# A fused attention, state-space and expert kernel: values and keys projected in four column blocks, with edits in the opening, the state-space stage and the experts

## The chip, the cores and the metric

The kernel is one program on one core of a Trainium2 chip. Its time is the device time of one launch in microseconds, beginning to end. The engines are PE (TensorE, matrix products; its weight loads are listed as PEld), DVE (VectorE), ACT (ScalarE), POOL (GpSimd) and SP (SyncE, which here only issues DMAs).

## The reference, cut to what matters

```python
# x: (16, 64, 128), ctx: (16, 1601, 128), all float32
q = layernorm(x) @ Wq.T + bq                   # 16 heads of 8
k, v = ctx @ Wk.T + bk, ctx @ Wv.T + bv
x = x + (softmax(q @ k.T / sqrt(8)) @ v) @ Wo.T + bo       # head by head
u = layernorm(layernorm(x)) * ln1_w + ln1_b
z, xBC, dt = in_proj(u); xs, Bm, Cm = silu(causal_conv4(xBC))
h = exp(dt * A) * h + dt * xs (x) Bm;  y = h . Cm + D * xs   # a scan over 64 tokens, 4 heads of 64
x1 = layernorm(x) + rmsnorm(y * silu(z)) @ out_proj
x = x + x1 + mlp(layernorm(x1))                # 512 wide, gelu
w = softmax(top2(dist(x, centroid)))           # 8 experts, each 342 wide
x = x + sum_e w_e * ((silu(x @ Wg + bg) * (x @ W1 + b1)) @ W2 + b2)
```

## The kernel before, in words

**Precision.** Products that must be exact to about float32 are made of three bf16 products (`product3`: high by high, high by low, low by high), the high and low halves made by ACT or POOL.

**Tiling.** The context of one batch lies as 128 features by 1601 tokens. Attention runs in 16 rounds, one a batch, of 13 steps, one for each 128 tokens of the context. In step k of round i, PE computes the scores of the 128 tokens (`scores`, eight matmuls, four groups of heads by two halves), ACT takes their exponentials into `probs`, and two steps later PE multiplies `probs` with the values and adds up in `sums` (`sum_values`): 16 float32 matmuls, four groups of four that write four different blocks of 32 columns of the array. The softmax needs each query's maximum before its scores, so a further pair of matmuls, a unit of `maxima`, makes 802 of the scores of batch i + 1 or i + 2 in a PSUM buffer and DVE reduces it (line 880); there are 16 units a batch. `turn_max` turns the maxima, DVE makes shifts of them, and these go into the rows of `q_cur` by DMA.

**The buffers handed to and fro.** `wide` is one PSUM tensor with two slots of 1024 columns. Everything that PE makes for another engine beside scores takes the two slots in turn; `RING` (from `ring_order`) numbers the uses, and `half_free` makes PE wait until the use before last was emptied. A slot is filled with a unit of maxima (emptied by DVE, about 1 us), half of the values of batch i + 2 (`vals`, 7 or 6 blocks of 128 tokens, 21 or 18 matmuls; copied by DVE), half of the keys of batch i + 3 (`keys`, two blocks of 401 tokens, six matmuls; copied by ACT), or a turn. `V_STEPS = (2, 5)`, `K_STEPS = (6, 8)` (9 and 11 in round 0) say in which steps they come: in the order of a step, scores, the first unit, the sum, further units, values, turn, keys.

**The opening.** Before round 0 the keys and values of batches 0 and 1, the keys of batch 2 and all queries are made. `score` and `sums` are not yet in use and serve as four spare PSUM banks: `make_spare` fills them in the order `SPARE_FIRST`, then `SPARE_LATER`, whose first 12 entries stand one behind each unit of maxima of batch 0 and whose last four (the keys of batch 2, emptied by ACT) stand behind the turn. The DMA that brings the shift of batch 0 into `q_cur` is issued by ACT's queue.

**Other queues.** POOL splits each context (2.9 and 3.2 us) and each batch's keys into high and low halves, in program order. SP issues in fixed steps the next context's load (`C_STEP`), and the copies of the split keys into `k_stack` (`H_STEP`, `L_STEP`), 1.6 MB and more a round. The program itself also comes over DMA: the page's queues q8 and q14 have the kind "instruction".

**State-space and MLP stage.** `mamba_mlp` works on tiles of two batches (128 tokens). DVE scans gains of 1024 elements four times (`gain`, line 1516), multiplies them with the product of Cm and Bm into `mix` (line 1525), PE sums `dtx` by `mix` (line 1224), DVE adds D * xs (line 1538) and multiplies with the gate.

**Experts.** A half of an expert is 512 tokens. For each of three blocks of 114 hidden units PE makes gate and up (`up`, six bf16 matmuls of 512 columns), ACT takes silu, DVE the product `hid_e`; and 12 float32 matmuls of 128 columns (24 records in the trace, since each passes twice) bring the half before down (`finish`, in two parts, line 1698), which DVE weighs and adds. Experts 1 to 6 run in a loop of two.

## Time and profile before

| | us |
|---|---|
| median of 3 runs (608.32 to 609.47) | 608.58 |
| the profiled execution, and its span | 609.61, 607.8 |
| opening, to the first scores | 55.8 |
| 16 attention rounds | 346.8 |
| state-space and MLP, with the routing | 87.2 |
| experts | 118.0 |
| busy: PE, PEld | 533.9, 353.5 |
| busy: DVE, ACT, POOL | 424.9, 358.3, 257.7 |

The mean granted clock of PE is 0.94 of 2.4 GHz. How the rows below are read. A window has its start and end, its length, the busy time and number of instructions of PE, PEld, DVE, ACT and POOL, PE's granted clock as a share, the busy share of the DMA engines (summed from modelled times, so it can pass 1), and GB/s. A row of the timeline has start, length, engine, line, operation, what is written and read, the shape, how many instructions were put together, and in brackets the idle time before it with what ended it; "issue" is idle time in which the engine waited for nothing that the profile shows. A row of the page's part 5 has a group's busy time, the mean of one in ns, the idle time before its instructions and what ended most of it. A DMA queue's row has packets, megabytes, and time as a share of 16 engines' span. Matmuls overlap: in a row of several the starts and not the lengths say how fast they pass.

### The profile page before, as it was taken

To read this page: it belongs to the slowest core of one execution; us is meant where nothing else is said; L and a number is where in the kernel's file an instruction comes from. 1 tells how busy PE (TensorE), PEld (TensorE's weight loads), DVE (VectorE), ACT (ScalarE), POOL (GpSimd) and SP (SyncE) were. 2 spreads that over 40 slices of the span, in tenths; PEclk is the share of its full clock that TensorE was granted. 3 is DMA by queue.
4 is the path that set the end of the run, shared out by engine and by line. 5 is a ranking of instruction groups with operands and counts; after the bars stand their busy time and mean duration, and the time that the engine had idled before them with its cause. 6 is when DMAs were issued, how large, how long until landed. Compare 5 with 4: busy or idle time off the path is not lost. (4 is left out here: it accounts for less than half of the span.)

```text
span 607.8 us, 17717 instructions
## 1 busy us (share of the span) xinstructions
PE 533.9 (88%) x7478; PEld 353.5 (58%) x7478; DVE 424.9 (70%) x754; ACT 358.3 (59%) x655; POOL 257.7 (42%) x137
## 2 busy tenths in 40 slices
PE   2795899999998899999999889977676979999997
PEld 1532655665565565566556556644465647777786
DVE  5174877888787788888878778347898565455454
ACT  4773476777677678777767759854813533233231
POOL 2694966658567467655854497022002000000000
PEclk9785899999999999999999889988758979999999
DMA  7794936965784684595557381011000000000001
GB/s 212 114 153 73 187 46 96 141 81 92 108 109 76 96 116 78 88 139 76 92 60 108 82 133 39 2 44 53 1 1 0 1 1 1 1 1 0 0 0 35
DMA packets 16405, 41.57 MB, mean 68 GB/s; under 512 B 3990, under 2 KB 6814, under 8 KB 16218
## 3 DMA queue, kind: packets, MB, share of 16 engines
q1 hardware_dynamic: 15592, 40.09, 40.2%
q8 instruction: 56, 0.92, 0.8%
q10 hardware_dynamic: 740, 0.42, 0.2%
q14 instruction: 17, 0.14, 0.1%
HBM read 19.70 MB, written 0.52 MB: 33 GB/s over the span
## 5 line engine op out<-in xcount | busy, mean ns | idle before, releaser
L880 DVE TENSOR_REDUCE half_max<-wide 128x2 f32<-128x802 f32 x256 | 241.7, 989 | 60.1 <-PE wide L570 56.4
L806 ACT ACTIVATE probs<-score 128x512 f32<-128x512 f32 (+1 forms) x416 | 225.8, 596 | 67.0 <-PE score L621 66.6
L641 PE MATMUL sums<-probs,values 128*32 128x192 f32 (+3 forms) x3328 | 133.4, 279 | 3.9 <-issue 3.9
L641 PEld LDWEIGHTS sums<-probs,values 128*32 128x32 f32 (+1 forms) x3328 | 87.2, 109 | 57.8 <-issue 27.3
L570 PE MATMUL wide<-k_stack,q_cur 48*128 48x401 bf16 x512 | 89.0, 346 | 8.8 <-issue 4.2
L621 PE MATMUL score<-q_cur,k_stack 50*128 50x128 bf16 (+1 forms) x1664 | 84.3, 221 | 12.0 <-ACT probs L806 5.0
L621 PEld LDWEIGHTS score<-q_cur,k_stack 50*128 50x128 bf16 (+1 forms) x1664 | 51.5, 96 | 43.5 <-issue 14.5
L1753 ACT ACTIVATE gate<-gu,gate_bias 114x512 f32<-114x512 f32 x48 | 32.9, 687 | 68.3 <-PE gu L1719 65.1
L405 POOL TENSOR_TENSOR ctx_hi<-ctx_in,one 128x1601 bf16<-128x1601 f32 x15 | 42.9, 2859 | 70.5 <-PE wide L492 61.7
L1838 DVE SCALAR_TENSOR_TENSOR hid_e<-gu,keep_bgu,gate 114x512 f32<-114x512 f32 x48 | 36.0, 751 | 51.9 <-ACT gate L1753 51.9
L417 POOL TENSOR_TENSOR k_hi<-k_full,one 128x1601 bf16<-128x1601 f32 x15 | 42.9, 2857 | 52.9 <-ACT k_full L788 38.6
L1698 PEld LDWEIGHTS down<-keep_w,hid_e 114*128 114x128 f32 x384 | 47.6, 192 | 3.6 <-DVE hid_e L1838 0.4
L408 POOL TENSOR_TENSOR ctx_lo<-ctx_in,ctx_hi 128x1601 bf16<-128x1601 f32 x15 | 48.6, 3243 | 1.2
L420 POOL TENSOR_TENSOR k_lo<-k_full,k_hi 128x1601 bf16<-128x1601 f32 x15 | 48.5, 3236 | 1.2
L1698 PE MATMUL down<-keep_w,hid_e 114*128 (+1 forms) x384 | 47.9, 275 | 0.2 <-DVE hid_e L1838 0.2
L788 ACT ACTIVATE k_full<-wide,keep_vecs 128x802 f32<-128x802 f32 x26 | 24.2, 930 | 31.6 <-PE wide L492 31.6
L570 PEld LDWEIGHTS wide<-k_stack,q_cur 48*128 48x128 bf16 x512 | 25.2, 95 | 28.4 <-DVE half_max L880 15.7
L876 DVE COPY values<-wide 128x896 f32<-128x896 f32 (+1 forms) x28 | 28.7, 1025 | 15.8 <-PE wide L492 15.8
L1717 PE MATMUL gu<-keep_t_hi,keep_w_hi 128*114 128x512 bf16 x96 | 37.2, 388 | 1.8 <-DVE hid_e L1838 1.8
L490 PE MATMUL wide<-wkv_hi,ctx_hi 128*128 128x128 bf16 x182 | 33.2, 224 | 4.3 <-DVE half_max L880 4.3
L1719 PE MATMUL gu<-keep_t_hi,keep_w_lo 128*114 128x512 bf16 x96 | 36.8, 384 | 0.0
L1718 PE MATMUL gu<-keep_t_lo,keep_w_hi 128*114 128x512 bf16 x96 | 36.8, 384 | 0.0
(290 smaller groups left out, 725.4 us busy)
## 6 DMA issues: line engine op xcount, KB each, us to landing
k_stack<-k_hi SPq DMA_DIRECT2D x64, 204.0 KB, 6.4
ctx_in<-in_ctx SPq DMA_DIRECT2D x56, 200.1 KB, 6.2
k_stack<-k_lo SPq DMA_DIRECT2D x32, 204.0 KB, 8.6
ctx_in<-in_wgu SPq DMA_DIRECT2D x16, 171.0 KB, 4.4
keep_w<-in_w SPq DMA_DIRECT2D x1, 1368.0 KB
ctx_in<-in_ctx SPq DMA_DIRECT2D x1, 800.5 KB, 8.4
keep_x<-in_x SPq DMA_DIRECT2D x1, 512.0 KB, 6.8
out<-keep_x SPq DMA_DIRECT2D x2, 256.0 KB, 2.3
```

Of the source, the lines that this page charges most:

```text
L405: pool.tensor_tensor(ctx_hi[:, n, 0:LK], ctx_in[:, n, :], one[:].to_broadcast([P, LK]), ALU.mult).then_inc(s_splithi, 1)
L408: pool.tensor_tensor(ctx_lo[:, n, 0:LK], ctx_in[:, n, :], ctx_hi[:, n, 0:LK], ALU.subtract).then_inc(s_split, 1)
L417: pool.tensor_tensor(k_hi[:, 0:LK], k_full[:, 0:LK], one[:].to_broadcast([P, LK]), ALU.mult).then_inc(s_khi, 1)
L420: pool.tensor_tensor(k_lo[:, 0:LK], k_full[:, 0:LK], k_hi[:, 0:LK], ALU.subtract).then_inc(s_klo, 1)
L570: last = pe.matmul(wide[:, w, 512 * p:512 * p + CH], q_cur[half:half + TERM, b % NQ, g].rearrange("p h q -> p (h q)"), k_stack[half:half + ...
L621: last = pe.matmul(score[0:m, (2 * step + p) % NSCORE, P * g:P * g + P], k_stack[half:half + TERM + 2, n, g, k * P:k * P + m], q_cur[half: ...
L641: last = pe.matmul(sums[32 * g:32 * g + 32, first * LQ:(first + heads) * LQ], values[0:m, n, k, VW * g + 2 * c:VW * g + 2 * c + 32], probs ...
L806: nc.scalar.activation(probs[0:m, step % NPROB, :].rearrange("r (g p c) -> r p g c", g=G, p=2)[:, p], score[0:m, (2 * step + p) % NSCORE, ...
L880: dve.tensor_reduce(half_max[:, b % 2, :, u // 4, u % 4], wide[:, w, :].rearrange("p (c k) -> p c k", c=2)[:, :, 0:CH], AX.X, ALU.max).the ...
L1698: last = pe.matmul(down[:, h, P * t:P * t + P], hid[:, h, n, P * t:P * t + P], keep.w2[:, bass.ds(e, 1), n, :].rearrange("p e c -> p (e c) ...
L1717: pe.matmul(o, hi, t_hi[:, half], start=True, stop=False)
L1718: pe.matmul(o, hi, t_lo[:, half], start=False, stop=False)
```

## The change

- **Values and keys in the rounds.** `keys` and `vals` call `columns3` instead of `product3`: each matmul of 128 output columns of the array becomes four of 32, that write four blocks of 32 partitions. Each output is made of the same three products in the same order. `make_spare` in the opening keeps `product3`.
- **Order in a step.** Values and keys stand after the sum and ahead of a step's further units of maxima. Values of batch 2 move from round 0 to the time between the turn of batch 0 and the first scores.
- **Opening.** The queries' first two groups come ahead of the maxima, and the last four spare jobs, the keys of batch 2, stand behind units 12 to 15 of the maxima and no longer behind the turn.
- **State-space stage.** Tokens of one batch only see each other, so the two batches of a tile are laid one under the other: gains, scan and mix have 64 columns where they had 128. The term D * xs becomes matmuls with a diagonal matrix ahead of the sums (`skipped`), the sum of the squares on POOL becomes two matmuls, and a scan's start is set by a bias on ACT and no longer by memsets on POOL.
- **Experts.** ACT makes the high half of `hid_e` (`high`), POOL the low half (`low`) and the halves of w2 (`split`), and the down product becomes 36 bf16 matmuls for a half of an expert in place of 12 float32 ones; its two parts stand at other places in the stream.

The core of the diff:

```diff
-    order += [("m", 0, u) for u in range(16)] + [("t", 0, 0)]
+    order += [("m", 0, u) for u in range(16)] + [("t", 0, 0), ("v", 2, 0), ("v", 2, 1)]
     for i in range(B):
         for k in range(NK):
-            order += [("m",) + unit for unit in units_at(i, k)]
-            if k in V_STEPS and i + 2 < B:
+            order += [("m",) + unit for unit in units_at(i, k)[:1]]
+            if k in V_STEPS and 0 < i < B - 2:
                 order += [("v", i + 2, V_STEPS.index(k))]
+            order += [("k",) + half for half in keys_at(i, k)]
+            order += [("m",) + unit for unit in units_at(i, k)[1:]]
             if k == turn_step(i) and i + 1 < B:
                 order += [("t", i + 1, 0)]
-            order += [("k",) + half for half in keys_at(i, k)]
...
+            def columns3(out, lhs_hi, lhs_lo, rhs_hi, rhs_lo):
+                for n, (lhs, rhs) in enumerate(((lhs_hi, rhs_hi), (lhs_hi, rhs_lo), (lhs_lo, rhs_hi))):
+                    for c in range(4):
+                        at = slice(32 * c, 32 * c + 32)
+                        last = pe.matmul(out[at], lhs[:, at], rhs, start=(n == 0), stop=(n == 2))
+                return last
...
-                    last = product3(wide[:, w, 512 * c:512 * c + CH], wkv_hi[:, 0, :], wkv_lo[:, 0, :],
+                    last = columns3(wide[:, w, 512 * c:512 * c + CH], wkv_hi[:, 0, :], wkv_lo[:, 0, :],
...
-                    last = product3(wide[:, w, at:at + P], ctx_hi[:, n, ks], ctx_lo[:, n, ks],
+                    last = columns3(wide[:, w, at:at + P], ctx_hi[:, n, ks], ctx_lo[:, n, ks],
...
                 maxima(0, u)
-                if u < 12:
+                if u < 10:
                     make_spare(SPARE_LATER[u])
+                elif u >= 12:
+                    make_spare(SPARE_LATER[u - 2])
             pe.wait_ge(s_nident, 16)
             turn_max(0)
-            for what in SPARE_LATER[12:]:
-                make_spare(what)
+            for half in range(2):
+                vals(2, half)
...
+                    if k in V_STEPS and 0 < i < B - 2:
+                        vals(i + 2, V_STEPS.index(k))
+                    for half in keys_at(i, k):
+                        keys(*half)
                     for unit in units[1:]:
                         maxima(*unit)
-                    if k in V_STEPS and i + 2 < B:
-                        vals(i + 2, V_STEPS.index(k))
                     if k == turn_step(i) and i + 1 < B:
                         turn_max(i + 1)
-                    for half in keys_at(i, k):
-                        keys(*half)
...
+            for half in range(2):
+                vals_out(2, half)
...
-            for h in range(2):
-                pool.wait_ge(s["ysq"], 2 * h + 2)
-                pool.tensor_tensor(y_sq[:, 0, half(h)], y_sq[:, 0, half(h)], y_sq[:, 1, half(h)],
-                                   ALU.add).then_inc(s["yss"], 1)
...
+            def skipped(h2):
+                pe.wait_ge(s["bcc"], 4)
+                pe.wait_ge(s["silu"], 4 * h2 + 2)
+                for b in range(2):
+                    for c in range(2):
+                        pe.matmul(y_out(h2, b, c), keep.skip[:, c, :],
+                                  xbc[:, c, half(h2)].rearrange("p (t b q) -> p t b q", b=2, q=LQ)[:, :, b, :],
+                                  start=(c == 0), stop=False, skip_group_check=True)
+            skipped(0)
             for h2 in range(2):
-                pe.wait_ge(s["bcc"], 4)
-                pe.wait_ge(s["dtx"], 4 * h2 + 4)
                 for t in range(4):
                     pe.wait_ge(s["mix"], 4 * h2 + t + 1)
+                    pe.wait_ge(s["dtx"], 4 * h2 + t + 1)
                     for h in range(MH):
                         r = 64 * (h % 2)
-                        last = pe.matmul(ps[r:r + 64, YA_SLOT[h2], 512 * (h // 2) + P * t:512 * (h // 2) + P * t + P],
-                                         dtx[:, 4 * h2 + t, 64 * h:64 * h + 64], mix[:, 4 * h2 + t, h, :],
-                                         start=True, stop=True)
+                        for b in range(2):
+                            rows = slice(LQ * b, LQ * b + LQ)
+                            last = pe.matmul(y_out(h2, b, h // 2)[r:r + 64, t, :],
+                                             dtx[rows, 4 * h2 + t, 64 * h:64 * h + 64], mix[rows, 4 * h2 + t, h, :],
+                                             start=False, stop=True, skip_group_check=True)
                 last.then_inc(s["ya"], 1)
+                if h2 == 0:
+                    skipped(1)
...
+                if c == 1:
+                    nc.scalar.activation(root_of[:], ones[:], ACT.Sqrt)
...
-                    count(dve.scalar_tensor_tensor(out=y[:, c, half(h)], in0=xbc[:, c, half(h)],
-                                                   scalar=vecs[:, V_D + c:V_D + c + 1],
-                                                   in1=ps[:, YA_SLOT[h], half(c)], op0=ALU.mult, op1=ALU.add))
-                    settle()
-                    dve.tensor_tensor(y[:, c, half(h)], y[:, c, half(h)], zg[:, c, half(h)],
-                                      ALU.mult).then_inc(s["yc"], 1)
+                    def by_batch(buf):
+                        return buf[:, c, half(h)].rearrange("p (t b q) -> p b t q", b=2, q=LQ)
+                    got = ps[:, YA_SLOT[h], :].rearrange("p (b c t q) -> p c b t q", b=2, c=2, q=LQ)[:, c]
+                    dve.tensor_tensor(by_batch(y), got, by_batch(zg), ALU.mult).then_inc(s["yc"], 1)
...
+        hid_hi = sb("hid_hi", [HT, 2, 2, NH, 512], BF16)
+        hid_lo = sb("hid_lo", [HT, 2, 2, NH, 512], BF16)
+        w2_hi = sb("w2_hi", [HT, E, NH, P], BF16)
+        w2_lo = sb("w2_lo", [HT, E, NH, P], BF16)
...
+                        hi, lo = hid_hi[:, par, h, n, P * t:P * t + P], hid_lo[:, par, h, n, P * t:P * t + P]
+                        pe.matmul(o, hi, w_hi2[:, n, :], start=(n == 0), stop=False)
+                        pe.matmul(o, hi, w_lo2[:, n, :], start=False, stop=False)
+                        last = pe.matmul(o, lo, w_hi2[:, n, :], start=False, stop=(n == NH - 1))
...
+                    if n == 0 and before:
+                        finish(*before, 1)
+                    if n == NH - 1 and prev:
+                        finish(*prev, 0)
...
+            def split(e):
+                got = of_expert(keep.w2, e)
+                pool.tensor_tensor(of_expert(w2_hi, e), got, one[:].unsqueeze(2).to_broadcast([HT, NH, P]),
+                                   ALU.mult).then_inc(s["w2s"], 1)
+                pool.wait_ge(s["w2s"], e * 2 + 1)
+                pool.tensor_tensor(of_expert(w2_lo, e), got, of_expert(w2_hi, e), ALU.subtract).then_inc(s["w2s"], 1)
+            def low(e, h, par, prev, before):
+                for n in range(NH):
+                    pool.wait_ge(s["hi"], e * 6 + (3 * h + n + 1))
+                    if isinstance(e, int) and e == E - 1 and h == 1 and n == NH - 1:
+                        return
+                    pool.tensor_tensor(hid_lo[:, par, h, n, :], hid[:, n, :], hid_hi[:, par, h, n, :],
+                                       ALU.subtract).then_inc(s["lo"], 1)
+                if h == 1 and not isinstance(e, int):
+                    split(e + 1)
...
+            def high(e, h, par, n):
+                act.wait_ge(s["hid"], e * 6 + (3 * h + n + 3))
+                nc.scalar.copy(hid_hi[:, par, h, n, :], hid[:, n, :]).then_inc(s["hi"], 1)
...
+                    if n:
+                        high(e, h, par, n - 1)
+                    elif prev:
+                        high(*prev, NH - 1)
```

The order of PE in step 5 of round 1, from the scores of the step to the first product of the half of values (`wide<-wkv_hi,ctx_hi`; `sums` is the sum, `wide<-k_stack` a unit of maxima), before:

```order
L621 MATMUL score<-q_cur,k_stack 128x128 x8
L570 MATMUL wide<-k_stack,q_cur 128x401 x2
L641 MATMUL sums<-probs,values 32x192 x4
L641 MATMUL sums<-probs,values 32x64 x4
L570 MATMUL wide<-k_stack,q_cur 128x401 x2
L490 MATMUL wide<-wkv_hi,ctx_hi 128x128
L491 MATMUL wide<-wkv_lo,ctx_hi 128x128
L492 MATMUL wide<-wkv_hi,ctx_lo 128x128
```

and of the change:

```order
L635 MATMUL score<-q_cur,k_stack 128x128 x8
L584 MATMUL wide<-k_stack,q_cur 128x401 x2
L655 MATMUL sums<-probs,values 32x192 x4
L655 MATMUL sums<-probs,values 32x64 x4
L505 MATMUL wide<-wkv_hi,ctx_hi 32x128 x4
L505 MATMUL wide<-wkv_lo,ctx_hi 32x128 x4
L505 MATMUL wide<-wkv_hi,ctx_lo 32x128 x4
```

The second unit of maxima has gone behind the values, and each product is four matmuls of 32 columns.

PE at the end of the opening, from the twelfth unit of batch 0 on (`score` and `sums` are spare banks here: `xnT,wq` a group of queries, `ctx_hi,wkv_hi` one quarter of the keys of batch 2; `wide<-nident` is the turn), before:

```order
L570 MATMUL wide<-k_stack,q_cur 128x401 x2
L536 MATMUL score<-xnT,wq 128x512
L570 MATMUL wide<-k_stack,q_cur 128x401 x8
L578 MATMUL wide<-nident,row_max 16x128
L490 MATMUL score<-ctx_hi,wkv_hi 128x401
L491 MATMUL score<-ctx_lo,wkv_hi 128x401
L492 MATMUL score<-ctx_hi,wkv_lo 128x401
L490 MATMUL sums<-ctx_hi,wkv_hi 128x401
```

and of the change:

```order
L584 MATMUL wide<-k_stack,q_cur 128x401 x2
L550 MATMUL score<-xnT,wq 128x512
L584 MATMUL wide<-k_stack,q_cur 128x401 x6
L496 MATMUL score<-ctx_hi,wkv_hi 128x401
L497 MATMUL score<-ctx_lo,wkv_hi 128x401
L498 MATMUL score<-ctx_hi,wkv_lo 128x401
L584 MATMUL wide<-k_stack,q_cur 128x401 x2
L496 MATMUL sums<-ctx_hi,wkv_hi 128x401
L497 MATMUL sums<-ctx_lo,wkv_hi 128x401
L498 MATMUL sums<-ctx_hi,wkv_lo 128x401
L584 MATMUL wide<-k_stack,q_cur 128x401 x2
```

The four quarters of keys, behind the turn before, stand between the last units of maxima.

PE in the first expert's part ahead of the loop (`gu` gate or up, `down` the down product), before:

```order
L1718 MATMUL gu<-keep_t_lo,keep_w_hi 114x512
L1719 MATMUL gu<-keep_t_hi,keep_w_lo 114x512
L1717 MATMUL gu<-keep_t_hi,keep_w_hi 114x512
L1718 MATMUL gu<-keep_t_lo,keep_w_hi 114x512
L1719 MATMUL gu<-keep_t_hi,keep_w_lo 114x512
L1698 MATMUL down<-keep_w,hid_e 128x128 x6
L1717 MATMUL gu<-keep_t_hi,keep_w_hi 114x512
L1718 MATMUL gu<-keep_t_lo,keep_w_hi 114x512
```

and of the change:

```order
L1753 MATMUL down<-w_hi,hid_hi 128x128
L1754 MATMUL down<-w_lo,hid_hi 128x128
L1755 MATMUL down<-w_hi,hid_lo 128x128
L1772 MATMUL gu<-keep_t_hi,keep_w_hi 114x512
L1773 MATMUL gu<-keep_t_lo,keep_w_hi 114x512
L1774 MATMUL gu<-keep_t_hi,keep_w_lo 114x512
L1772 MATMUL gu<-keep_t_hi,keep_w_hi 114x512
L1773 MATMUL gu<-keep_t_lo,keep_w_hi 114x512
L1774 MATMUL gu<-keep_t_hi,keep_w_lo 114x512
L1753 MATMUL down<-w_hi,hid_hi 128x128
L1754 MATMUL down<-w_lo,hid_hi 128x128
```

Between the groups of six first products stood six float32 matmuls at a time; now the down products stand in groups of three bf16 ones for each block, and in other gaps.

## Rows read from the trace of the kernel before

**Rows 1.** Windows by stage: engines' busy time (count), granted clock, DMA share, GB/s

```profile
0.00:55.80 55.80, 35.42 (x180) 17.61 (x180) 26.36 (x53) 31.98 (x74) 29.32 (x22) 0.80 0.74 141
55.80:402.60 346.80, 322.47 (x6246) 204.95 (x6246) 272.89 (x361) 249.53 (x457) 217.97 (x100) 0.98 0.59 91
...
489.80:607.80 118.00, 112.04 (x704) 86.89 (x704) 59.46 (x153) 36.18 (x61) 0.00 (x0) 0.98 0.02 5
```

**Rows 2.** Part 5 of the page, costliest group of VectorE

```profile
L880 DVE TENSOR_REDUCE half_max<-wide 128x2 f32<-128x802 f32 x256 | 241.7, 989 | 60.1 <-PE wide L570 56.4
```

**Rows 3.** Timeline, PE, a step and the step after

```profile
222.80 0.40 PE L621 MATMUL score<-q_cur,k_stack 50*128 50x128 bf16 x8
223.03 0.34 PE L570 MATMUL wide<-k_stack,q_cur 48*128 48x401 bf16 x2
223.29 0.64 PE L641 MATMUL sums<-probs,values 128*32 128x192 f32 x16
223.87 0.23 PE L490 MATMUL wide<-wkv_hi,ctx_hi 128*128 128x128 bf16 x1
...
224.98 0.23 PE L621 MATMUL score<-q_cur,k_stack 50*128 50x128 bf16 x2
225.56 0.34 PE L621 MATMUL score<-q_cur,k_stack 50*128 50x128 bf16 x6 [0.35 <-issue]
```

**Rows 4.** Timeline, PE, at a stop

```profile
202.82 0.53 PE L641 MATMUL sums<-probs,values 128*32 128x192 f32 x7
204.52 0.43 PE L641 MATMUL sums<-probs,values 128*32 128x192 f32 x9 [1.17 <-issue]
```

**Rows 5.** Windows between stops, of a block, and of a quiet stretch

```profile
183.72:204.52 20.80, 18.86 (x382) 12.05 (x382) 17.70 (x22) 15.09 (x28) 12.36 (x6) 1.00 0.61 89
204.52:225.56 21.04, 19.63 (x383) 12.47 (x383) 16.40 (x21) 14.82 (x27) 12.37 (x7) 1.00 0.60 88
197.20:204.52 7.32, 6.08 (x131) 3.98 (x132) 6.55 (x7) 4.34 (x8) 1.97 (x1) 1.00 1.06 135
336.60:358.46 21.86, 20.44 (x382) 12.59 (x382) 17.58 (x21) 15.09 (x28) 16.20 (x8) 0.92 0.57 90
372.60:378.00 5.40, 5.40 (x138) 3.54 (x130) 5.07 (x7) 4.80 (x10) 3.78 (x2) 1.00 0.02 5
```

**Rows 6.** Part 3 of the page, and the DMA view of 200.80 to 202.70

```profile
q8 instruction: 56, 0.92, 0.8%
...
q8 instruction: 1, 0.02, 6.0%
```

**Rows 7.** Windows, one round in two parts

```profile
258.30:272.30 14.00, 13.28 (x265) 8.74 (x264) 11.67 (x15) 9.73 (x19) 7.84 (x5) 1.00 0.99 142
272.30:279.90 7.60, 7.26 (x143) 4.20 (x138) 6.14 (x10) 6.20 (x12) 6.19 (x3) 1.00 0.06 19
```

**Rows 8.** Timeline, PE in the experts; then part 5 of the page

```profile
528.83 1.50 PE L1698 MATMUL down<-keep_w,hid_e 114*128 x12
530.17 0.38 PE L1717 MATMUL gu<-keep_t_hi,keep_w_hi 128*114 128x512 bf16 x1
...
L1753 ACT ACTIVATE gate<-gu,gate_bias 114x512 f32<-114x512 f32 x48 | 32.9, 687 | 68.3 <-PE gu L1719 65.1
L408 POOL TENSOR_TENSOR ctx_lo<-ctx_in,ctx_hi 128x1601 bf16<-128x1601 f32 x15 | 48.6, 3243 | 1.2
```

**Rows 9.** Timeline, state-space stage: DVE, then PE

```profile
441.14 2.28 DVE L1516 TENSOR_TENSOR_SCAN gain<-decay_all,keep_delta 128x1024 f32<-128x1024 f32 x1
443.45 1.28 DVE L1525 TENSOR_TENSOR mix<-gain,ps 128x512 f32<-128x512 f32 x2
...
453.97 0.75 DVE L1538 SCALAR_TENSOR_TENSOR y<-xbc,keep_vecs,ps 128x512 f32<-128x512 f32 x1
...
450.42 5.48 PE L1224 MATMUL ps<-mix,keep_sums 128*64 128x128 f32 x64
```

**Rows 10.** Timeline, PE, the first scores

```profile
55.82 0.39 PE L621 MATMUL score<-q_cur,k_stack 50*128 50x128 bf16 x4 [3.12 <-DMA q_cur<-shift]
```

More of the change, by code:

```diff
@@ L985, in _ @@
                             row_maxima(b)
-                    if k in V_STEPS and i + 2 < B:
+                    if k in V_STEPS and 0 < i < B - 2:
                         vals_out(i + 2, V_STEPS.index(k))
+                    for b, u in units[1:]:
+                        maximum(b, u)
+                        if u == 15:
+                            row_maxima(b)
                     if k == turn_step(i) and i + 1 < B:
@@ L1056, in mamba_mlp @@
         names = ("w turn o ot otc att x1 st var sq u ln vt vtc dtp dts dte mm conv silu zin zsil "
-                 "ones dp dpt dpc tsp cen dots tap bc bcc bc0 scan cb mix xt dtx ya yc ysq yss out r rq y1 "
+                 "ones dp dpt dpc tsp cen dots tap bc bcc scan cb mix xt dtx ya yc ysq out r rq y1 "
                  "fc gelu pr")
@@ L1176, in spread @@
                     for h in range(MH):
-                        last = pe.matmul(ps[:, BC_SLOT[c], P * (MH * t + h):P * (MH * t + h) + P],
-                                         sel[:, h, :], decayT[:, tok(2 * c + t)], start=True, stop=True)
+                        at = LQ * (MH * t + h)
+                        for b in range(2):
+                            first = P * (2 * c + t) + LQ * b
+                            last = pe.matmul(ps[LQ * b:LQ * b + LQ, BC_SLOT[c], at:at + LQ],
+                                             sel[:, h, 0:LQ], decayT[:, first:first + LQ], start=True, stop=True)
                 last.then_inc(s["bc"], 1)
@@ L1200, in overlap @@
                 for t in range(4 * h, 4 * h + 4):
-                    last = pe.matmul(ps[:, CB_SLOT, tok(t)], xbc[0:64, 2, tok(t)], xbc[0:64, 3, tok(t)],
-                                     start=True, stop=True)
+                    for b in range(2):
+                        first = P * t + LQ * b
+                        last = pe.matmul(cb_out(t)[LQ * b:LQ * b + LQ, :],
+                                         xbc[0:64, 2, first:first + LQ], xbc[0:64, 3, first:first + LQ],
+                                         start=True, stop=True)
                 last.then_inc(s["cb"], 1)
@@ L1236, in _ @@
                                          start=(c == 0), stop=(c == 1))
-                pe.wait_ge(s["yss"], h + 1)
+                pe.wait_ge(s["ysq"], 2 * h + 2)
                 for t in range(4 * h, 4 * h + 4):
-                    last = pe.matmul(bank(6 + h)[:, t:t + 1], y_sq[:, 0, tok(t)], ones[:], start=True, stop=True)
+                    for c in range(2):
+                        last = pe.matmul(bank(6 + h)[:, t:t + 1], y_sq[:, c, tok(t)], ones[:],
+                                         start=(c == 0), stop=(c == 1))
                 last.then_inc(s["out"], 1)
@@ L1325, in _ @@
             gate_silu(0)
+            act.wait_ge(s["ones"], 1)
             for c in range(4):
@@ L1622, in experts @@
         small = pb("small", [P, 2, 512])
-        names = "w gb sp nrm rt top te sel weT wtc gu gate hid down acc b2"
+        names = "w one gb sp nrm rt top te sel weT wtc gu gate hid hi lo w2s down acc b2"
         s = {n: sem("e_" + n) for n in names.split()}
@@ L1657, in per_expert, with of_expert @@
             body(E - 1, 1, False)
+            last()
+        def of_expert(buf, e):
+            return buf[:, bass.ds(e, 1)].rearrange("p e n c -> p (e n) c")
         @block.sync
@@ L1720, in up, with last_ones, _ @@
                     last.then_inc(s["gu"], 1)
-                    if between and n:
-                        between(n - 1)
-            per_expert(pe, up, finish, route)
+                    if n == 0 and before:
+                        finish(*before, 1)
+                    if n == NH - 1 and prev:
+                        finish(*prev, 0)
+            def last_ones():
+                finish(E - 1, 0, 1, 1)
+                finish(E - 1, 1, 1, 0)
+                finish(E - 1, 1, 1, 1)
+            per_expert(pe, up, last_ones, route)
+        @block.gpsimd
+        def _(pool):
+            pool.memset(one[:], 1.0).then_inc(s["one"], 1)
+            pool.wait_ge(s["one"], 1)
+            def split(e):
[13 more added lines that the diff above has]
+                    split(e + 1)
+            pool.sem_inc(s["lo"], 3)
+            split(0)
+            split(1)
+            per_expert(pool, low, lambda: None, lambda step: None)
         @block.scalar
@@ L1740, in route, with gates @@
                                        small[0:E, h, :]).then_inc(s["wtc"], 1)
-            def gates(e, h, par, between):
+            def high(e, h, par, n):
+                act.wait_ge(s["hid"], e * 6 + (3 * h + n + 3))
+                nc.scalar.copy(hid_hi[:, par, h, n, :], hid[:, n, :]).then_inc(s["hi"], 1)
+            def gates(e, h, par, prev, before):
                 if h == 0:
@@ L1831, in weigh, with hidden @@
                 last.then_inc(s["acc"], 1)
-            def hidden(e, h, par, between):
+            def hidden(e, h, par, prev, before):
                 for n in range(NH):
```

116 lines of the change are left out of this document (65 added, 51 removed).

## The prediction

> **What bounds the kernel now.** I read first the stages by windows. The opening ends at 55.8, the attention rounds take the 346.8 us to 402.6 (57% of the span), the experts the last 118, and the state-space and MLP stage stands between them [rows 1]. The profiled execution took 609.61 us around a span of 607.8; the median of the runs shown is 608.58, so terms measured in the profile are taken off the median.
>
> In the rounds PE and DVE are both near full: 322.5 and 272.9 us of 346.8. The costliest group is DVE's row maxima, 989 ns each [rows 2], 16 a round: 15.8 us. With two copies of values of about 1 us each and the small work of a shift I estimate 18.9 us in a round; a round lasts 346.8 over 16, 21.7, the undisturbed ones 21.3. The order of time shows what PE does in a step: a score group, a pair of maxima and a sum of values take 1.08 us together (222.80 to 223.87) [rows 3]. Thirteen of these are 14.0 us; two halves of values (1.1 and 1.0), two of keys (six matmuls of 401 columns at 2.4 GHz, 1.03 each), three more maxima (0.26 each), and a turn with the changes of the array's shape (some 1.0) give about 19.9. So PE has some 1.6 us of room in a round and DVE some 2.5; neither alone is the bound, for they hand two buffers to and fro.
>
> The reader is then to see a wait of another kind. At 203 us PE stops inside a sum of values, in the middle of one group that waits for no semaphore, and goes on at 204.52; "issue" stands beside it [rows 4]. The same stands at 225.56 [rows 3]. Between those two ends PE ran 383 matmuls and 383 weight loads, 766 instructions; between the end at 183.72 and that at 204.52, 382 and 382 [rows 5]. The page has 56 packets of kind "instruction" with 0.92 MB, 16.4 KB each [rows 6]; 14,956 PE instructions over 56 is 267 to a packet. So PE's program comes in blocks of some 256 instructions, three to a stretch between stalls (768 against 764 and 766, the rest being branch and semaphore instructions), and a stall falls at a block's edge. The block of 197.20 to 204.52 took 7.32 us; its packet is on the queue only in the stretch from 200.80 to 202.70, 3.6 us after the edge at which it could first be wanted [rows 5, 6]. Data traffic explains the lateness: in the first 14 us of a round the DMA engines are 99% busy, in the rest 6% [rows 7]. With no traffic (372.60 to 378.00) 268 instructions pass in 5.4 us and nothing stalls [rows 5].
>
> **The change, part by part.**
>
> *Values and keys in four blocks of columns.* Each matmul of 128 columns becomes four of 32. In streaming nothing is lost: the sums of values are such groups of four already, and 16 of their matmuls pass in 0.58 us (223.29 to 223.87), where eight of 192 columns in two passes and eight of 64 would need 1.7 us one after another, so they do run beside each other [rows 3]. Half a step of values, 21 matmuls in 1.11 us, should become 84 in 1.1 to 1.2. The switches of shape beside a sum of values go away, about 0.09 us each (a pair of maxima streams 0.17 us and the sum starts 0.26 after it, 223.03 to 223.29), perhaps three a round, 0.3 us; since DVE and not PE closes the round, I count this as nothing.
>
> What grows is the program. A round has 39 matmuls of values and 12 of keys; they become 156 and 48, 153 more, and with their weight loads 306 more instructions on some 780 (764 and 766 in 20.80 and 21.04 us, scaled to 21.3). That is 4.3 blocks a round where 3.1 were. All of it falls in the first nine steps, just where DMA is busy: nine steps of 52 instructions (26 matmuls and their loads), 312 for the values and 96 for the keys are 876 in 13.9 us of PE work, so a block is used up in 4.1 us there, and one that is fetched in traffic needed 7.3 [rows 5, 7]. Each such block makes PE wait 3.2 us. Two such blocks fit into 14 us of traffic: 6.4 us a round, less the 1.6 of room, 4.8. If only one of them is that late, 1.6 remain. Twelve full rounds (the last ones load no values) give 19 to 58 us; I take the middle, 38. At the lower end outside this, the fetch stays hidden and the term is nothing.
>
> *Values of batch 2 ahead of the rounds, keys of batch 2 within the maxima, two query groups earlier.* PE waits at 55.82 for the shift's DMA for 3.12 us [rows 10], and that DMA was issued on ACT's queue behind the last four copies of keys. Now these copies come before the turn, and the values fill the wait. I take 4 us off the opening and 3 off round 0, which loses two halves of values at half clock: minus 7, between minus 10 and minus 3. Queued behind the moved keys is the rest of the maxima: were context 2 not split by then, DVE would stand idle with them.
>
> *State-space stage.* The scan goes from 1024 to 512 elements: 2.28 us each becomes 1.14; the mix pair 1.28 becomes about 0.8 [rows 9]. Four times 1.6 is 6.5 us of DVE. But PE's order of turns and overlaps stays and holds DVE up (each pair of turned tiles comes after its spread), so I count 3.5. The skip term leaves DVE (four of 0.75) [rows 9] and becomes eight float32 matmuls of 256 columns and four passes, 0.43 us each at 2.4 GHz and 0.85 at 1.2, on PE in line ahead of the sums, where the clock stood at half until about 453; the second half of the skip now also stands ahead of the first output projection. The 64 records of the old sum took 5.48 us [rows 9]; in quarters of the array they stream half as long. The sum on POOL goes, eight more one-column matmuls come, and a table load moves off the path. I count minus 2.5 in all, between minus 7 and plus 4.
>
> *Experts.* 12 down records take 1.34 us (528.83 to 530.17), and nothing on PE waits [rows 8]. A half of an expert costs 18 first products of 512 columns at 2.4 GHz, 0.216 each, 3.89, and 24 down records, 2.68: 6.57. Down becomes 36 bf16 matmuls of 128 columns at the 0.056 us at which the values' matmuls follow each other (21 from 223.87 to 224.98, less the switch) [rows 3], 2.0. ACT gains three copies, estimated at 0.6 each, beside three gates of 0.69: 3.9 of 5.9. DVE keeps what it has. POOL's three low parts and its share of the weights' split come to about 4.3, by its 3.24 us for 1601 elements [rows 8]. All stay under PE's 5.9. Sixteen halves give 0.67 each, 10.7, and a tail longer by the copy and the low part, about 0.5: minus 10, between minus 12 and minus 6.
>
> **The sum.** 608.6 - 7 - 2.5 - 10 + 38 = 627.
>
> **Rivals.**
> A. The blocks arrive in time. For it: only one block in three is late today, and a stall costs 1.5 us at most. Then the rounds stay at DVE's pace and the time is 608.6 - 19.5 = 589. The Trainium skill's page "Runtime: NRT & Kernel Launch", section "Instruction fetch mechanics", has this rule: the next block of 256 instructions is fetched while one is executed, and the cost of an edge is mostly hidden. By that rule alone the time would be this 589; rows 4 and 5 show edges that cost over a microsecond.
> B. No late blocks, but small matmuls have a floor from start to start. A score group's eight take 0.23 us (222.80 to 223.03), 29 ns each; a sum's 16 take 36 ns each [rows 3]. At 29 ns for every start the halves of values take 2.4 and 2.1 us, 2.4 us more a round, or 0.8 to 2.4 after the room: 10 to 31 us, 600 to 620, say 610. Against it: in groups of narrow blocks four starts seem to share one slot. The skill's page "TensorE: Matmul & The Clock Gate", section "Wait — 56ns, not 53.3ns?", gives about 25 ns as the least distance of two starts; by it 84 would take 2.1 us, and no row here shows a long run of narrow ones.
> C. Late blocks and, after them, half the clock. The stretch after the stall that ended at 336.60 ran at 0.92 of the clock [rows 5]. A dozen falls of about 1 us on top of the upper half of the term: 640 to 655.
> D. The opening's moved keys wait for the split of context 2 and the early gain is lost, with the rest as forecast: 634.
>
> **How the numbers follow.** My forecast 0.50, C 0.12, D 0.05, B 0.15, A 0.18. What a measurement of this kernel can tell from no change is 0.2%, 1.2 us. Faster is A and the low part of B: 0.20. Same: 0.03. Slower: 0.77. The range runs from 597, which leaves out A, to 648, which takes in most of the term's upper end. The forecast's own range is 610 to 646.
>
> **What would show it.** The rounds' stage should take some 380 us instead of 346.8, with over 20 waits of PE marked "issue" of 1 to 3 us, nearly all in the first two thirds of a round, and 71 to 75 instruction packets instead of 56. Windows between these waits should hold multiples of 256 instructions. DVE's idle time before its maxima should grow by the same 35 us. An experts' half should take 5.9 us; the first score should come near 52. The forecast is wrong if the rounds last under 350 us with 70 and more packets (A), or if the value halves themselves stretch evenly to 2 us (B).

## The result, and the profile after

The changed kernel takes 658.94 us, median of 4 runs (655.08 to 660.43), against 609.03 for the kernel before on the same chip: 1.080 times as long, 95% interval 1.074 to 1.086. The forecast was 627, its range 597 to 648.

The stages by windows in the changed kernel (columns as in [rows 1]); the last two windows are a half of an expert in the loop, and the experts' first 15.4 us from the first product on:

```profile
0.00:52.12 52.12, 33.80 (x372) 18.26 (x372) 27.56 (x54) 31.37 (x74) 32.28 (x23) 0.93 0.82 157
52.12:462.20 410.08, 336.77 (x8197) 215.91 (x8196) 273.24 (x362) 249.69 (x458) 216.49 (x101) 0.92 0.48 77
462.20:544.90 82.70, 66.01 (x492) 45.54 (x493) 56.51 (x183) 39.13 (x64) 6.87 (x11) 0.78 0.05 18
544.90:657.20 112.30, 103.35 (x896) 74.26 (x896) 64.00 (x154) 60.88 (x109) 68.13 (x64) 0.96 0.02 6
...
581.88:587.78 5.90, 5.90 (x57) 4.30 (x55) 3.36 (x8) 3.58 (x7) 4.10 (x4) 1.00 0.00 0
546.60:562.00 15.40, 12.80 (x57) 7.01 (x58) 8.66 (x37) 8.26 (x16) 7.25 (x7) 0.79 0.01 2
```

Against [rows 1] the opening is 3.7 us shorter, the rounds are 63.3 us longer, the state-space and MLP stage 4.5 us and the experts 5.7 us shorter: 49.4 us longer in all, as the spans have it (657.2 and 607.8). So the rounds alone make the loss. In them DVE is busy for 273.24 us as before (272.89), its maxima take as long as before, and PE has 14 us more of busy time; most of what grew is time in which PE and DVE stand still, and the granted clock fell from 0.98 to 0.92.

The waits of PE in the changed kernel, largest first (us in total, times, longest), then rows of the page: DVE's maxima, its copies of values (L876 before, L892 after), and three of the DMA queues:

```profile
PE wide L505 <- issue: 24.1, 11, 4.3
PE sums L655 <- issue: 19.9, 6, 4.6
PE score L635 <- issue: 9.7, 3, 3.9
```

```profile
L896 DVE TENSOR_REDUCE half_max<-wide 128x2 f32<-128x802 f32 x256 | 243.0, 989 | 85.0 <-PE wide L584 81.0
...
L876 DVE COPY values<-wide 128x896 f32<-128x896 f32 (+1 forms) x28 | 28.7, 1025 | 15.8 <-PE wide L492 15.8
L892 DVE COPY values<-wide 128x896 f32<-128x896 f32 (+1 forms) x28 | 28.7, 1024 | 49.7 <-PE wide L505 49.7
...
q8 instruction: 75, 1.23, 0.9%
q10 hardware_dynamic: 740, 0.42, 0.2%
q14 instruction: 19, 0.15, 0.1%
```

Twenty waits for nothing that the profile shows, 53.7 us; nineteen of them, 51.5 us, lie in the rounds, and one of 2.25 at the end of the opening. The kernel before had seven in its rounds, 6.9 us, the longest 1.6. There are 75 packets of q8 where [rows 6] has 56. DVE's wait before the maxima grew by 24.9 us (85.0 for the 60.1 of [rows 2]) and that before its copies of values by 33.9 (49.7 for 15.8): it waits for what the stopped PE has not made (35 before the maxima alone had been forecast). That PE's stops stand at the edges of blocks of 256 instructions is to be read from two stops that follow one another and from the window between their ends:

```profile
251.89 0.23 PE L505 MATMUL wide<-wkv_hi,ctx_hi 128*32 128x128 bf16 x2 [3.62 <-issue]
...
272.92 0.51 PE L655 MATMUL sums<-probs,values 128*32 128x192 f32 x3
278.00 1.07 PE L655 MATMUL sums<-probs,values 128*32 128x192 f32 x13 [4.57 <-issue]
279.01 0.61 PE L635 MATMUL score<-q_cur,k_stack 50*128 50x128 bf16 x8
279.41 0.54 PE L584 MATMUL wide<-k_stack,q_cur 48*128 48x401 bf16 x2
```

```profile
251.89:278.00 26.11, 20.28 (x509) 12.66 (x510) 16.93 (x21) 14.82 (x27) 14.02 (x6) 0.91 0.50 74
```

It holds 509 matmuls and 510 loads, 1019 of the 1024 of four blocks (the rest are branch and semaphore instructions or missing records). The lateness of the packet shows in the DMA view. From 269.40, the edge before, to 274.60 there is only data on the queues, 103.4% of the engines' time; the packet comes in the stretch from 274.60 to 276.50:

```profile
q1 hardware_dynamic: 231, 0.61, 103.4%
```

```profile
q1 hardware_dynamic: 82, 0.24, 108.5%
q8 instruction: 1, 0.02, 5.8%
```

PE had used up its block at 273.4, in 4.0 us (the forecast's 4.1), stopped inside a sum of values, and went on at 278.00. Behind the stop the same instructions take longer: a score group passes in 0.40 us (279.01 to 279.41) and not in the 0.23 of [rows 3]. The clock was at its lower level, 1.2 GHz, in the whole of the first window below, and the second shows it back at 2.4:

```profile
276.70:283.50 6.80, 5.50 (x121) 4.00 (x120) 1.57 (x2) 1.13 (x3) 0.47 (x1) 0.50 0.23 54
...
283.50:290.30 6.80, 5.84 (x134) 3.39 (x132) 4.55 (x7) 5.31 (x9) 5.92 (x3) 1.00 0.22 60
```

And the narrow matmuls themselves, in a half of values at the full clock: four of them start in every 0.055 us, the pace at which the prediction has one of 128 columns pass (0.056). A half of values still takes some 1.2 us.

```profile
216.94 0.23 PE L505 MATMUL wide<-wkv_hi,ctx_lo 128*32 128x128 bf16 x4
217.00 0.23 PE L505 MATMUL wide<-wkv_hi,ctx_hi 128*32 128x128 bf16 x4
217.06 0.23 PE L505 MATMUL wide<-wkv_lo,ctx_hi 128*32 128x128 bf16 x4
217.11 0.23 PE L505 MATMUL wide<-wkv_hi,ctx_lo 128*32 128x128 bf16 x4
```

### The profile page after: what moved, and what is told of

It is laid out like the page before. It is cut to its first block and busy times, and to the rows that moved or that the text cites. A ratio compares the mean times of both kernels' runs of the same rounds, so it can differ in the third digit from the quotient of the medians.

```text
span 657.2 us, 22953 instructions
## 1 busy us (share of the span) xinstructions
PE 539.9 (82%) x9956; PEld 354.0 (54%) x9956; DVE 421.3 (64%) x751; ACT 381.1 (58%) x704; POOL 323.8 (49%) x197
## 5 line engine op out<-in xcount | busy, mean ns | idle before, releaser
L655 PE MATMUL sums<-probs,values 128*32 128x192 f32 (+3 forms) x3328 | 141.5, 292 | 21.7 <-issue 19.9
L655 PEld LDWEIGHTS sums<-probs,values 128*32 128x32 f32 (+1 forms) x3328 | 90.9, 114 | 81.5 <-issue 49.9
L584 PE MATMUL wide<-k_stack,q_cur 48*128 48x401 bf16 x512 | 92.9, 360 | 11.7 <-ACT k_full L804 6.3
L635 PE MATMUL score<-q_cur,k_stack 50*128 50x128 bf16 (+1 forms) x1664 | 88.0, 228 | 16.4 <-issue 9.7
L635 PEld LDWEIGHTS score<-q_cur,k_stack 50*128 50x128 bf16 (+1 forms) x1664 | 55.1, 99 | 44.1 <-issue 19.8
L1805 POOL TENSOR_TENSOR hid_lo<-hid_e,hid_hi 114x512 bf16<-114x512 f32 x47 | 54.1, 1157 | 36.2 <-ACT hid_hi L1833 35.2
L892 DVE COPY values<-wide 128x896 f32<-128x896 f32 (+1 forms) x28 | 28.7, 1024 | 49.7 <-PE wide L505 49.7
L505 PE MATMUL wide<-wkv_hi,ctx_hi 128*32 128x128 bf16 x728 | 39.3, 238 | 12.7 <-issue 9.8
L505 PE MATMUL wide<-wkv_lo,ctx_hi 128*32 128x128 bf16 x728 | 39.3, 238 | 6.3 <-issue 6.3
L505 PE MATMUL wide<-wkv_hi,ctx_lo 128*32 128x128 bf16 x728 | 38.9, 238 | 3.8 <-issue 3.8
L804 ACT ACTIVATE k_full<-wide,keep_vecs 128x802 f32<-128x802 f32 x26 | 24.1, 929 | 28.2 <-PE wide L505 28.2
```

Source lines behind the costliest of these rows:

```text
L505: last = pe.matmul(out[at], lhs[:, at], rhs, start=(n == 0), stop=(n == 2))
L584: last = pe.matmul(wide[:, w, 512 * p:512 * p + CH], q_cur[half:half + TERM, b % NQ, g].rearrange("p h q -> p (h q)"), k_stack[half:half + ...
L635: last = pe.matmul(score[0:m, (2 * step + p) % NSCORE, P * g:P * g + P], k_stack[half:half + TERM + 2, n, g, k * P:k * P + m], q_cur[half: ...
L655: last = pe.matmul(sums[32 * g:32 * g + 32, first * LQ:(first + heads) * LQ], values[0:m, n, k, VW * g + 2 * c:VW * g + 2 * c + 32], probs ...
L1805: pool.tensor_tensor(hid_lo[:, par, h, n, :], hid[:, n, :], hid_hi[:, par, h, n, :], ALU.subtract).then_inc(s["lo"], 1)
```

## The experiments

Theory F: the program's blocks come late behind the data of a round, and there are more of them. Rivals: the new order in a step (O), and the small matmuls by themselves, by their starts or by the clock (S). A second question came from the first runs: what a stop costs beyond its own length (theory H: the clock is at half for a while after it).

**e1_plain.** Plain products in keys and vals, the rest of the change kept.

```diff
-                    last = columns3(wide[:, w, 512 * c:512 * c + CH], ...
+                    last = product3(wide[:, w, 512 * c:512 * c + CH], ...
-                    last = columns3(wide[:, w, at:at + P], ctx_hi[:, n, ks], ...
+                    last = product3(wide[:, w, at:at + P], ctx_hi[:, n, ks], ...
```

> The changed kernel with product3 in keys and vals: no narrow blocks in the rounds, the rest of the change stays. Theory F (the program's blocks come late in the DMA traffic of a round, and there are more blocks): the stops go back to those of the kernel before, the rounds to 340 to 347 us, and with the opening, the state-space stage and the experts as in the profile after (3.7, 4.5 and 5.7 us shorter) the time is 589 to 596. Rival O (the new place of values and keys ahead of the second unit of maxima makes DVE and PE wait for each other): the rounds stay above 390 us, time 640 or more.

Measured 593.95 (592.99 to 595.24), ratio to before 0.973, 0.969 to 0.978. The rounds take 347.58 us with a clock of 0.98, and PE waits for "issue" 8.3 us:

```profile
PE sums L655 <- issue: 4.3, 4, 2.3
PE score L635 <- issue: 4.0, 2, 2.1
```

O falls as the cause of the loss. The rounds of the changed kernel are 62.5 us longer than these (410.08 less 347.58), 43.2 of them in stops (51.5 in its rounds, less 8.3).

**e2_before_columns.** The kernel before with `columns3` in the two calls, nothing else.

```diff
-                    last = product3(wide[:, w, ...
+                    last = columns3(wide[:, w, ...
```

> The kernel before with columns3 in keys and vals of the rounds and nothing else. Theory F: rounds of 400 to 415 us, some 20 stops marked issue of 1 to 5 us, 75 instruction packets less those of the other stages (about 72), time 660 to 672. Rival O: no more than 615, since the order is that of before.

Measured 676.48 (673.77 to 678.81), 1.110, 1.105 to 1.116: a little over the top of the expectation. The rounds take 408.6 us, with 48.8 us of "issue" in 18 waits at the three places shown. This one edit makes the whole loss; the rest of the change gains 14 to 18 us with it or without it (608.31 less 593.95, 676.48 less 658.94).

```profile
PE wide L499 <- issue: 20.5, 9, 4.7
PE sums L649 <- issue: 18.6, 6, 4.5
PE score L629 <- issue: 9.7, 3, 4.1
```

**e4_filler.** Plain products, and tiny matmuls that nobody reads make the program as long as the changed one.

```diff
+            def filler(w, blocks):
...
+                for n in range(9 * blocks):
+                    c = n % 4
+                    at = slice(32 * c, 32 * c + 32)
+                    last = pe.matmul(wide[at, w, 1016 + n // 4 % 4:1017 + n // 4 % 4], wkv_hi[:, 0, at],
+                                     wkv_hi[:, 1, 0:1], start=True, stop=True)
+                return last
```

> The changed kernel with product3 in keys and vals, and behind each half as many more tiny matmuls as columns3 would add (32 columns of the array, one column moving, into PSUM columns that nobody reads; 153 a round with their loads): the program has the length of the changed one, the streaming that of the plain one. Theory F: the stops come back, time 645 to 662. Rival S: within 10 us of the kernel with plain products, under 606.

Measured 675.59 (671.13 to 676.91), 1.108, 1.103 to 1.114. The stops come back, 41.3 us of them in rounds of 424.2, with work that streams almost nothing. That it is 17 us slower than the changed kernel had not been expected. An estimate from the trace: 63 fillers take 0.56 us (308.14 to 308.70, shape switch included), so 153 some 1.4 us a round and 18 us in all, where narrow blocks take no time more than wide ones. Its stops are 10 us less than the changed kernel's and its rounds 14 us longer, so the fillers explain most of the 24 us between and not all.

```profile
308.14 0.63 PE L513 MATMUL wide<-wkv_hi 128*32 128x1 bf16 x63
308.70 0.40 PE L647 MATMUL score<-q_cur,k_stack 50*128 50x128 bf16 x8
```

**e3_spread.** The changed kernel; SP issues a round's ten DMAs of 0.2 MB one a step.

```diff
-H_STEP, L_STEP, C_STEP = 1, 3, 5
+H_STEPS, L_STEPS, C_STEPS = (0, 1, 2, 3), (4, 5), (6, 7, 8, 9)
```

> The changed kernel with the ten big DMAs of a round issued one a step (high halves at steps 0, 1, 2, 3, low halves at 4, 5, context at 6 to 9) in place of 2, 2, 2 at steps 0, 1, 3 and context at 5 to 8. Same program, same bytes. Theory F: a queue in front of the instruction packets is then at most one DMA deep (about 1.4 us in place of 3 to 6), most stops shrink below 1 us, the rounds take 345 to 370 us and the time is 592 to 620. Rival S (the number of small matmuls costs by itself, by starts or by a clock that falls under them): nothing changes, 650 to 662.

Measured 619.91 (619.34 to 620.83), 1.016, 1.011 to 1.021. The same program and the same bytes, 39 us less than the changed kernel. The rounds take 371.80 us at a clock of 0.96; the whole trace has 26 stops at the places shown, 28.2 us (25.8 of them in the rounds), and the longest is 3.2:

```profile
PE wide L507 <- issue: 14.8, 13, 3.2
PE sums L657 <- issue: 10.0, 8, 2.5
PE score L637 <- issue: 3.4, 5, 2.0
```

So the queue ahead of a packet is what counts, and the number of packets alone does not. Of the 26 stops 16 are under 1 us, as had been expected of most; ten of 1.1 to 3.2 us remain. The rounds stay 33.0 us above those of e5 below, the same spreading with plain products; 22.9 of that is in stops.

**e6_light.** The changed kernel; from batch 3 on only 256 of the 1632 columns of the split keys are copied. The rest of the copy is left out, so the result is not the right one.

```diff
+                cols = LKS if b < NSLOT else 256
...
-                        sp.dma_start(k_stack[at:at + PAIR, n, :, :], k_hi[half:half + 64, :]).then_inc(done, 16)
+                        sp.dma_start(k_stack[at:at + PAIR, n, :, 0:cols], k_hi[half:half + 64, 0:cols]).then_inc(done, 16)
```

> The changed kernel, narrow blocks and all, but from batch 3 on only 256 of the 1632 columns of the split keys are copied into k_stack (the rest is what an earlier batch left there, a part of the computation that is left out). Same program of PE, 1.0 MB less traffic a round; the four context loads at steps 5 to 8 stay. Theory F: the stops in steps 1 to 4 go, a few at steps 5 to 9 stay; rounds 345 to 360 us, time 592 to 610. Rival S (the length of the program costs by itself, with the traffic or without): 650 or more.

Measured 585.91 (582.95 to 587.2), 0.963, 0.957 to 0.969, below the range given. All 153 added matmuls of a round are there, the DMA share is 0.22, 2.3 us of stops are left in the rounds, and these last 336.83 us:

```profile
51.67:388.50 336.83, 313.27 (x8201) 203.54 (x8196) 271.83 (x361) 249.59 (x458) 216.83 (x101) 0.98 0.22 53
```

S falls. Here the cost of the narrow blocks is gone, as the forecast's rival A had it; it needs quiet DMA queues.

**e8_light_plain.** The same with plain products.

> Plain products (product3), and from batch 3 on only 256 of the 1632 columns of the split keys copied (part of the computation left out): the pair of the run with narrow blocks in light traffic (585.9). Theory F with DVE's pace as the bound of the rounds: narrow blocks save or cost nothing once the program arrives in time, so 583 to 588. If narrow blocks save PE time that counts (the switches of the array's shape, 0.3 us a round or more), this one is 4 us or more slower, 590 up; if they cost by themselves, 582 or less.

Measured 583.92 (581.66 to 584.9), 0.961, 0.958 to 0.964; rounds 335.77. Its rounds have no wait for "issue". Even where the program is hardly ever late, the edit of keys and vals saves nothing: 585.91 with it, 583.92 without.

**e7_keys_columns.** Narrow blocks in the keys alone.

> Narrow blocks in the keys only: 36 matmuls more in a round and not 153, some 0.3 of a block of 256 instructions. Theory F goes by program length: about 3.4 blocks a round for 3.1 and 4.3, so a quarter of the way from 594 to 659, 600 to 615. If the narrow blocks cost by themselves and by their streaming (401 columns each), half of the way or more, 625 up.

Measured 602.62 (600.53 to 606.92), 0.993, 0.989 to 0.996; 62 packets, rounds 355.74. By count of instructions a quarter of the way was asked, and 13% of it came (8.7 of 65 us). A few packets more cost less than in proportion, and the longer stops, with the half clock behind them, are still missing: the longest here is 2.6 us.

**e5_plain_spread and e9_before_spread.** The DMAs spread as in e3, in the kernel with plain products and in the kernel before.

> The kernel with plain products (product3) in keys and vals and the rest of the change, its big DMAs spread one a step. Theory F: its six stops (9.8 us in all beside 345 us of rounds) nearly go, but DVE's pace then holds the rounds (18.9 us of work in 21.3), so they get 2 to 7 us shorter: time 587 to 592. If the traffic's place cost nothing here, 592 to 596.

> The kernel before with its ten big DMAs spread one a step and nothing else. Theory F: its seven stops of 8.2 us in all and the two stretches at half clock go for the most part: 5 to 9 us less, 600 to 604. If they cost nothing there (hidden beside DVE), within 1.5 us of the kernel before.

Measured 586.81 (584.65 to 588.08), 0.966, 0.961 to 0.970, for the first, the fastest kernel here that computes everything; its rounds last 338.82 us. The second takes 600.46 (598.71 to 604.47), 0.989, 0.985 to 0.992: spreading gives it 8 us. Their rounds:

```profile
50.48:389.30 338.82, 313.81 (x6207) 200.88 (x6207) 271.74 (x361) 249.60 (x458) 217.82 (x101) 0.99 0.58 93
```

```profile
52.41:392.00 339.59, 318.59 (x6246) 203.45 (x6246) 272.76 (x362) 249.50 (x458) 217.89 (x100) 0.98 0.58 93
```

In e9 1.8 us of stops are left of 6.9, and the rounds are 7.2 us shorter (346.80 less 339.59): more than the stops alone.

**e10_hold.** e5 with PE stopped once a round by something other than its program.

```diff
+                if 1 <= i <= 12:
+                    sp.dma_start(hold[:], A["ident"]).then_inc(s_hold, 16)
...
+                    if k == L_STEPS[0] and 1 <= i <= 12:
+                        pe.wait_ge(s_hold, 16 * i)
                     scores(i, k)
```

> The kernel with plain products and spread DMAs (586.8) in which PE is stopped once a round in rounds 1 to 12 by something else than its program: the scores of step 4 wait for a small DMA of 64 KB that SP issues when the scores of step 3 are made. It asks what a stop costs beyond its own length. In the changed kernel the rounds lost 62.5 us against plain products, 48 of them in stops. Theory H (half clock after a stop costs the rest): the records show stretches of 3.4 us or more at half clock behind stops near 3 us and longer, and the rounds grow by the sum of the stops plus 0.5 to 1.5 us for each such stretch; with 12 stops of 2 to 4 us, 610 to 645. Rival: the stops cost their own sum or less (1.6 us of room a round takes a part), with the rest of the loss in the changed kernel then due to its narrow blocks.

Measured 657.61 (656.85 to 660.58), 1.075, 1.070 to 1.079: more than expected. The rounds' window and the wait:

```profile
51.63:462.40 410.77, 341.96 (x6207) 216.75 (x6207) 273.25 (x360) 249.45 (x458) 217.73 (x101) 0.89 0.44 79
```

```profile
PE score L641 <- DMA hold<-in_ident: 46.9, 12, 5.6
```

Against e5 the rounds grew by 72.0 us, the stops are 46.9, and 25.1 us come on top, 2.1 for each stop. A mean clock of 0.89 over 410.77 us is 90 us at half; in e5 (0.99 over 338.82) it is 7. If all that comes on top is put down to the clock, a microsecond at half clock cost 0.30. In the changed kernel 0.92 over 410.08 is 66 us, in e1 0.98 over 347.58 is 14; 52 more, 15.6 us by that price, where 19.3 are to be explained (62.5 less 43.2). The same division gives 0.37 in this pair, 0.39 in e2 against the kernel before (61.8 us of rounds, 41.8 of stops, 51 at half clock) and 0.44 in e3 against e5 (33.0, 22.9, 23). The clocks are rounded to a hundredth, which is up to 4 us at half in each, so these prices agree only roughly. They fit theory H. That the clock and not something else behind a stop costs this time is not shown: no run separates the two. A second reserve: e10's stops stand in step 4 alone, so its price is carried over from one place to others.

## Why the prediction was wrong

**What bounds the kernel: right.** Blocks of 256 instructions, late behind data traffic, in stops at "issue".

**Values and keys: the right mechanism, the size wrong.** The step that failed is the term's size: "Two such blocks fit into 14 us of traffic: 6.4 us a round, less the 1.6 of room, 4.8", and "I take the middle, 38". The term measured 65.0 us (658.94 less 593.95). Its stops nearly came out: a block was used up in 4.0 us, stops up to 4.6 us came, 20 in number with 75 packets (71 to 75 forecast). The middle of one late block a round and two, 3.2 and 6.4, is 58 us of stops in twelve rounds before the room is taken off; 43.2 came on top of e1's. What the runs showed in place of the rest is two terms. First, the room of 1.6 us a round, 19 in twelve, gave nothing back: the stops grew by 43.2 us and the rounds by more than that, 62.5; e9 shows the same from the other side, where 5.1 us less of stops made the rounds 7.2 shorter. A likely reason, which no run tests, is that a stop empties the chain of two buffers between PE and DVE for both, and that DVE, with an estimated 18.9 us of work in a round of 21.2 (e5 and e9), has little time to make up. Second, the half clock behind the stops, which the forecast left out of the term and kept for rival C at "A dozen falls of about 1 us". [Rows 5] had it in sight: after the stop that ended at 336.60 the clock was 0.92. With stops two to three times as long it was the rule and not the exception, and cost 16 us by e10's price, 19 if all that is left over is its. So C, at 0.12, was the case that came, 4 us above its upper end; the forecast should have made the half clock a part of the likeliest case. In the changed kernel the clock fell during or behind each of the eleven stops of 2.9 us and more, in e10 at all twelve; in e2 three of 2.9 to 3.0 us went by without.

**Opening: minus 7 forecast, minus 6.9 measured.** The first score stands at 52.12, where 52 was forecast, 3.7 us earlier. Round 0 gave 3.2 more, with 3 forecast: the first score of round 1 stands 27.4 us after that of round 0 before, and 24.3 after the change. The same row shows it in both kernels, before first:

```profile
83.22 0.40 PE L621 MATMUL score<-q_cur,k_stack 50*128 50x128 bf16 x8 [0.22 <-ACT probs L806]
```

```profile
76.37 0.40 PE L635 MATMUL score<-q_cur,k_stack 50*128 50x128 bf16 x8 [0.23 <-ACT probs L822]
```

PE waited 1.2 us for the split of context 2, far from the 7 of rival D, which falls. The values of batch 2 were themselves stopped:

```profile
41.12 0.49 PE L496 MATMUL score<-ctx_hi,wkv_hi 128*128 128x401 bf16 x1 [1.20 <-POOL ctx_lo L410]
...
51.26 0.23 PE L505 MATMUL wide<-wkv_lo,ctx_hi 128*32 128x128 bf16 x1 [2.25 <-issue]
```

**State-space stage: minus 2.5 forecast, minus 4.5 measured.** DVE's scans went nearly as worked out, and DVE then waited for PE, as feared:

```profile
495.36 1.22 DVE L1565 TENSOR_TENSOR_SCAN gain<-decay_all,keep_delta 128x512 f32<-128x512 f32 x1 [1.39 <-ACT decay_all L1379]
496.72 0.75 DVE L1574 TENSOR_TENSOR mix<-gain,ps 128x256 f32<-128x256 f32 x2
...
510.04 1.29 DVE L1591 TENSOR_TENSOR y<-ps,zg 128x512 f32<-128x512 f32 x2 [2.92 <-PE ps L1264]
```

```profile
505.18 3.62 PE L1251 MATMUL ps<-xbc,keep_skip 128*128 128x256 f32 x8
508.73 1.17 PE L1264 MATMUL ps<-mix,keep_sums 64*64 64x64 f32 x64
```

The scan fell from 2.28 to 1.22, the mix pair from 1.28 to 0.75, and the sums from 5.48 [rows 9], the first 3 us of it at half clock, to two times 1.17 at full clock; the skip product takes 3.62 at half clock in front of the first.

**Experts: minus 10 forecast, minus 5.7 measured.** A half in the loop takes 5.90 us, with 5.9 forecast, for 6.57: twelve of them give 8. The four other halves and the tail took 2.3 back and were forecast to give some 2. At the start PE waited 3.9 us for `hid_e` (1.8 before), and the clock was 0.79 in the first 15.4 us (0.91 in the same stretch before); which of the two came first is open.

**The rest of the change together.** Minus 19.5 was forecast; e1 has minus 14.4 (608.31 to 593.95). In its trace rounds 1 to 15 are 4.1 us longer than in the kernel before, with 1.4 us more of stops; no run takes the new order of a step out by itself, so this cost is open. The forecast's miss of 32 us is then 27 from the term of values and keys and 5 from here.

**Rivals.** B: four starts in 0.055 us, and fillers every 0.009 us; no floor near 25 or 29 ns from start to start was met, so that rule of the Trainium skill's page "TensorE: Matmul & The Clock Gate" (section "Wait — 56ns, not 53.3ns?") does not hold for blocks of columns. A: its mechanism holds under light traffic only, where narrow blocks and plain ones differ by 2 us (e6 and e8). That e6 takes 586, near the 589 worked out, is in part luck: light traffic also took 10 us off the kernel with plain products (593.95 to 583.92), and the rest of the change gave 5 us less than the 589 counts on. The Trainium skill's page "Runtime: NRT & Kernel Launch", section "Instruction fetch mechanics", calls the cost of a block's edge mostly hidden. The traces agree for quiet queues (2.3 us of stops in e6's rounds, with 75 packets) and are against it for full ones (51.5 us, with as many).

## What to carry to other kernels

An instruction is paid for in program bytes as well as in time: where DMA queues are full, a block of 256 PE instructions may come over 5 us late (269.4 to 274.6 above), and a stretch that uses one up faster than that will stop. Look at "issue" waits of the busiest engine, count instructions between them, and spread the data DMAs before making the program longer. In e10 stops of 3.9 us cost 6 us each, their own length and, most likely, the half clock after it.

## What had not been expected of the hardware

Matmuls on different blocks of 32 columns follow each other every 14 ns with 128 columns moving (four in 0.055 us), and every 9 ns with one column moving (63 in 0.56 us). Ten DMAs of 0.2 MB spread over a round, the same bytes, took 39 us off the changed kernel, 7 off the one with plain products and 8 off the kernel before. Twelve stops of 3.9 us that had nothing to do with the program cost 6.0 us each.
